# A selective scan: dt's maximum, B's diagonals and the mean's subtraction moved from VectorE to ScalarE and GpSimd

## The chip, the cores and the metric
One Trainium2 chip, 8 NeuronCores. Each core computes one sequence of the batch of 8, with no communication. The metric is the device time in microseconds of the slowest core. A core has TensorE (matmul, PE in the profile), VectorE (DVE), ScalarE (ACT), GpSimd (POOL) and SyncE (SP, here it only starts DMAs). Each works through its own queue of instructions in order; semaphores tie the queues together.

## The reference, cut to what matters
One layer of four parts: a Mamba block, a feed-forward block, attention, and the feed-forward block again, each with a layernorm ahead of it and a residual. Only the Mamba block is touched:
```python
# x: [2048 tokens, 1024] per core, after layernorm (x - mean) / sqrt(var + eps)
xb, zb = split(x @ in_proj_w)                 # 2048 channels each
xb = silu(conv4(xb)); zb = silu(zb)
dt, B, C = split(xb @ x_proj_w)               # 128, 16, 16
dt = softplus(dt @ dt_proj_w + dt_proj_b)     # per token and channel
h = exp(dt * A) * h + dt * B * xb             # 16 states per channel, scan over tokens
y = sum_n(C * h) + D * xb
out = (y * zb) @ out_proj_w
```

## The kernel before
The 2048 tokens are cut into four **quarters** q of 512, and the 2048 channels into 16 blocks c of 128. A **step** s = 16 q + c scans one block over one quarter; there are 64 steps. A step has 8 **slots** p, one for each pair of the 16 states (P = 8 s + p).

Work of one slot: ScalarE makes the two decays exp(dt A) of the pair after next (L910). TensorE multiplies the transposed v = dt * xb with diagonal matrices of B into PSUM (L921), for the next pair. VectorE runs the two scans of the pair (`tensor_tensor_scan`, L944), which read the decay from SBUF and the input from PSUM. After every second pair GpSimd copies the four last states for the next quarter (L956) and multiplies the four states with C (L959, 128x2048); TensorE sums those products over the states with identity matmuls (L1002) two slots later, in its queue behind the inputs of the next pair. VectorE multiplies the sum of a step with the gate in slot 3 of the next one (L1012). There are four buffers for states of two pairs, two for products.

dt of the next step is made inside a step: in slot 0 a matmul into a bank of PSUM (L853) and three passes on ScalarE: Relu (L857), Exp (L861), Ln (L865). They use softplus(u) = max(u, ln(1 + exp(min(u, 40)))), where min(u, 40) comes as 40 - relu(40 - u). In slot 2 VectorE takes the maximum with u, read from the bank (L875), which frees the bank, and GpSimd multiplies with xb for v (L880). In slot 4 TensorE transposes v (L890).

Between these, a list of **pieces** is spread over the slots of a step: projections of the next quarter (8 matmuls each, L587 and L685), gates, the output projection of the last quarter (L789, with the addition of x on VectorE, L803), and, in steps 0 to 2 of a quarter, the layernorm of the next. In its slot a piece comes last. The layernorm's eight tiles are applied in steps 1 and 2, four each: in quarter 0 in slots 0, 1, 4 and 6, in quarters 1 and 2 in slots 4 to 7. For one tile ScalarE copies x from SBUF to a PSUM bank (L562), VectorE subtracts the mean there (L568) and multiplies with 1/std into bf16 (L571). Step 14 of a quarter holds the x projection of the next, and at its end the 32 diagonal blocks of B (`dg`) in one VectorE operation (L761, 128x4096). In quarter 3 the pieces are passes of ScalarE over the feed-forward weights (|w|, L842, four a step), whose tiles SyncE loads into two buffers.

Three PSUM banks serve matmul pieces in turn (`take_bank`, `drop_bank`); if all three are held, late work is emitted early to free one. GpSimd's queue also starts weight-casting DMAs in slot 1 (L315): in steps 0 to 22, and then in every second step up to 30 (steps 0 to 2 have another in slot 5).

## Time and profile before
| | us |
|---|---|
| median of 3 runs | 3261.96 (3252.79 to 3271.25) |
| the profiled execution | 3267.86 |
| its slowest core (1), first to last instruction | 3266.2 |
| mean granted TensorE clock of that core | 0.885 of full speed |
| Mamba block, last gate product L1012 | starts at 1684.7 |

The profile was taken on core 1, and all rows below are that core's. Idle time stands behind an instruction in square brackets, with what ended it. "x4" is four instructions merged into one row. A row of the windows gives the stretch (start:end), its length, then the busy time (and instructions) of PE, PEld (weight loads), DVE, ACT and POOL, the granted clock, the DMA share and GB/s. Busy time on GpSimd there includes the starting of DMAs.

### The profile page before, as it was taken

To read this page: it belongs to the slowest core of one execution; us is meant where nothing else is said; L and a number is where in the kernel's file an instruction comes from. 1 tells how busy PE (TensorE), PEld (TensorE's weight loads), DVE (VectorE), ACT (ScalarE), POOL (GpSimd) and SP (SyncE) were. 2 spreads that over 40 slices of the span, in tenths; PEclk is the share of its full clock that TensorE was granted. 3 is DMA by queue.
4 is the path that set the end of the run, shared out by engine and by line. 5 is a ranking of instruction groups with operands and counts; after the bars stand their busy time and mean duration, and the time that the engine had idled before them with its cause. 6 is when DMAs were issued, how large, how long until landed. Compare 5 with 4: busy or idle time off the path is not lost.

```text
span 3266.2 us, 47261 instructions; the slowest of 8 cores (3212.5 to 3266.2 us)
## 1 busy us (share of the span) xinstructions
PE 2492.8 (76%) x16368; PEld 1159.3 (35%) x16368; DVE 1874.4 (57%) x1924; ACT 1863.5 (57%) x2713; POOL 1247.2 (38%) x622
## 2 busy tenths in 40 slices
PE   5555887678876876765564899899746887799999
PEld 2212332233322333322221344344534663344444
DVE  3267998799979999798853200421367765311001
ACT  2355886578866887788842653653222333563543
POOL 1246896588866887677740200200110000200000
PEclk8867998799988998877777899999878998899999
DMA  5567344645433112443344122131100112114323
GB/s 134 136 108 99 101 107 123 144 110 106 95 119 104 56 59 75 151 132 106 105 125 158 52 78 75 56 122 62 42 7 20 37 37 68 42 62 116 97 74 104
DMA packets 122616, 294.39 MB, mean 90 GB/s; under 512 B 16304, under 2 KB 24944, under 8 KB 119296
## 3 DMA queue, kind: packets, MB, share of 16 engines
q1 hardware_dynamic: 118480, 252.27, 25.3%
q0 software_dynamic: 3904, 39.09, 8.1%
q8 instruction: 137, 2.24, 0.3%
q14 instruction: 95, 0.78, 0.1%
HBM read 304.12 MB, written 60.00 MB: 111 GB/s over the span
## 4 chain that ended last, share of the span: by engine, by line
PE 50%; DVE 17%; ACT 13%; issue 10%; DMA 7%; SPq 1%; POOL 1%; DVEq 0%; ACTq 0%; POOLq 0%
PE ps L1403 13%; PE ps L1438 13%; DVE X L944 10%; ACT AR L910 6%; PE ps L1567 5%; PE ps L587 4%; PE ps L1002 4%; PE ps L789 2%; PE ps L921 2%; PE ps L1722 1%; ACT L910 1%; DVE AR L1263 1%; DMA AR<-x_fm 1%; PE ps L685 1%; DMA AR<-ip_bf 1%
## 5 line engine op out<-in xcount | busy, mean ns | idle before, releaser
L944 DVE TENSOR_TENSOR_SCAN X<-AR,ps 128x512 bf16<-128x512 f32 x1024 | 1208.9, 1244 | 132.6 <-PE ps L921 95.2
L959 POOL TENSOR_TENSOR AR<-X 128x2048 bf16<-128x2048 bf16 x256 | 1040.4, 4064 | 87.7 <-DVE X L944 81.1
L910 ACT ACTIVATE AR<-AR 128x512 f32<-128x512 f32 x1024 | 654.7, 711 | 6.5 <-DVE X L944 5.7
L921 PE MATMUL ps<-AR 64*128 64x128 bf16 x4096 | 221.8, 234 | 397.8 <-DVE X L944 373.4
L1403 PE MATMUL ps<-AR 128*128 128x512 bf16 x2048 | 463.4, 390 | 20.8 <-ACT AR L1331 13.4
L1438 PE MATMUL ps<-AR 128*128 128x512 bf16 x2048 | 445.1, 380 | 7.2 <-ACT AR L1331 7.2
L1194 POOL TENSOR_TENSOR AR<-X 128x512 f32<-128x512 f32 x8 | 10.1, 1264 | 1079.7 <-DVE AR L1263 689.1
L1460 DVE TENSOR_TENSOR X<-AR,X 128x512 f32<-128x512 f32 x64 | 43.6, 692 | 652.6 <-ACT AR L1452 652.6
L921 PEld LDWEIGHTS ps<-AR 64*128 64x128 bf16 x4096 | 134.4, 100 | 573.0 <-issue 571.6
L1002 PE MATMUL ps<-AR 128*128 128x512 bf16 x1024 | 323.3, 447 | 4.6 <-POOL AR L959 4.6
L1331 ACT ACTIVATE AR<-AR 128x1024 bf16<-128x1024 bf16 x256 | 258.0, 1046 | 117.0 <-DMA AR<-w2c 111.7
L587 PE MATMUL ps<-X,AR 128*128 128x512 bf16 x1024 | 280.6, 424 | 53.6 <-DMA AR<-ip_bf 27.5
L1403 PEld LDWEIGHTS ps<-AR 128*128 128x128 bf16 x2048 | 204.9, 100 | 282.3 <-issue 54.8
L1438 PEld LDWEIGHTS ps<-AR 128*128 128x128 bf16 x2048 | 200.4, 98 | 251.3 <-issue 11.8
L1567 PE MATMUL ps<-AR 128*128 128x256 bf16 x1536 | 199.4, 292 | 89.3 <-DVE AR L1584 31.3
L1413 ACT ACTIVATE AR<-ps,AR 128x1024 bf16<-128x1024 f32 x128 | 153.9, 1204 | 147.2 <-PE ps L1403 146.7
L1567 PEld LDWEIGHTS ps<-AR 128*128 128x128 bf16 x1536 | 155.6, 104 | 122.3 <-issue 94.6
L587 PEld LDWEIGHTS ps<-X,AR 128*128 128x128 bf16 x1024 | 106.2, 108 | 201.0 <-issue 113.5
L1452 ACT ACTIVATE AR<-ps,AR 128x512 f32<-128x512 f32 x64 | 46.3, 774 | 177.4 <-PE ps L1438 177.4
L956 POOL CAST AR<-X 128x4 f32<-128x4 bf16 x192 | 35.9, 187 | 279.5 <-DVE X L944 269.9
L1002 PEld LDWEIGHTS ps<-AR 128*128 128x128 bf16 x1024 | 94.5, 108 | 133.1 <-issue 62.3
L789 PE MATMUL ps<-AR 128*128 128x512 bf16 x512 | 129.7, 404 | 12.0 <-DMA AR<-op_bf 7.2
(136 smaller groups left out, 2493.9 us busy)
## 6 DMA issues: line engine op xcount, KB each, us to landing
X<-w SPq DMA_DIRECT2D x64, 512.0 KB, 3.7
AR<-w1c SPq DMA_DIRECT2D x128, 256.0 KB, 2.6
AR<-w2c SPq DMA_DIRECT2D x128, 256.0 KB, 3.1
AR<-ip_bf SPq DMA_DIRECT2D x112, 256.0 KB, 4.1
AR<-x_fm SPq DMA_DIRECT2D x80, 256.0 KB, 5.6
AR<-op_bf SPq DMA_DIRECT2D x32, 512.0 KB, 6.4
AR<-cdg SPq DMA_DIRECT2D x48, 256.0 KB, 3.5
X<-ip_pk SPq DMA_DIRECT2D x16, 512.0 KB, 3.7
```

The costliest lines, as they stand in the source:

```text
L587: f = lambda e, k=k: e.matmul(st["b"][1], wi[i][:, k, :], xn[q % 2][:, k, :], start=(k == 0), stop=(k == 7))
L789: f = lambda e, k=k: e.matmul(st["b"][1], wo[i][:, k, :], yz[(16 * q + k) % NYZ], start=(k == 0), stop=(k == 15))
L910: f = lambda e, n=n: e.activation(out=dec[P % 4][:, n, :], in_=dtt[s % 2], func=AF.Exp, scale=av[:, c, 2 * p + n:2 * p + n + 1])
L921: f = lambda e, tb=tb, h=h: e.matmul(self.bank(2 * (P % 2) + h)[:, tb * 128:tb * 128 + 128], vT[s % 2][64 * h:64 * h + 64, tb * 128:tb * 1 ...
L944: f = lambda e, n=n, init=init: e.tensor_tensor_scan(out=hh[J % 4][:, 2 * (P % 2) + n, :], data0=dec[P % 4][:, n, :], data1=src[:, :, n], ...
L959: S["hc", J] = tk("gp", lambda e: e.tensor_tensor(out=hc[J % 2], in0=hh[J % 4], in1=cbc[q % 2][:, 4 * j:4 * j + 4, :], op=ALU.mult))
L1002: f = lambda e, n=n: e.matmul(py, self.ident[:], hc[J % 2][:, n, :], start=False, stop=(j == 3 and n == 3))
L1331: u_ready[n] = tk("act", lambda e: e.sign(out=flat, in_=flat))
L1403: f = lambda e, k=k: e.matmul(pp[:, ch * 512:ch * 512 + 512], wu[n % NW][:, k, :], xn_h[:, k, ch * 512:ch * 512 + 512], start=(k == 0), st ...
L1413: ev[m] = tk("act", lambda e: e.activation(out=hact[:, m, :], in_=pp, func=AF.Gelu, scale=self.al1_t[:, m:m + 1], bias=self.b1_t[:, m:m + 1]))
L1438: e.matmul(pp[:, ch * 512:ch * 512 + 512], wu[n % NW][:, k, :], hact[:, kk, ch * 512:ch * 512 + 512], start=(kk == 0), stop=(kk == 31)))
L1567: f = lambda e, k=k: e.matmul(pb[:, 0:256], wts[i][:, j, k * 128:(k + 1) * 128], xu(w)[:, k, :], start=(k == 0), stop=(k == 7))
```

## The change
Three pieces of work leave VectorE.
1. softplus as a sum: u is at most 40 or not, so max(u, ln(1 + exp(min(u, 40)))) is written as relu(u - 40) + ln(1 + exp(min(u, 40))). ScalarE makes relu(u - 40) with a second Relu from the same bank (`zb`, one buffer, so it waits for the last step's addition), the bank is free after it, and GpSimd adds (L879 after the change) instead of VectorE's maximum.
2. B's diagonals: four operations of 128x1024 in place of one of 128x4096, each a piece of its own, on GpSimd from quarter 1 on (L759 after). A pair of states waits only for its quarter of them.
3. The mean: in quarters 1 to 3 GpSimd subtracts it in place in the SBUF tile of x (L561 after), and VectorE multiplies from there (L565 after). ScalarE's copy and the PSUM bank go.

```diff
         zb = alloc([128, TQ], F32)          # new
...
             def apply(k):
                 def main():
                     xk, ld, i = st["n", k]
-                    if q == 0:
-                        src = xk
-                        need("ve", ld)
-                    else:
-                        bi, src = take_bank()
-                        need("act", ld, bank_done[bi])
-                        c = tk("act", lambda e: e.activation(
-                            out=src, in_=xk, func=AF.Copy))
-                        r_xs.free[i] = (c,)
-                        need("ve", c)
-                    need("ve", S["ln_stat"], S.get(("z_in", q - 2)),
+                    eng = "ve" if q == 0 else "gp"
+                    need(eng, ld, S["ln_stat"])
+                    t = tk(eng, lambda e: e.tensor_tensor(
+                        out=xk, in0=xk, in1=mean, op=ALU.subtract))
+                    need("ve", t, S.get(("z_in", q - 2)),
                          S.get(("x_in", q - 2)))
                     t = tk("ve", lambda e: e.tensor_tensor(
-                        out=src, in0=src, in1=mean, op=ALU.subtract))
-                    need("ve", t)
-                    t = tk("ve", lambda e: e.tensor_tensor(
-                        out=xn[q % 2][:, k, :], in0=src, in1=rstd,
+                        out=xn[q % 2][:, k, :], in0=xk, in1=rstd,
                         op=ALU.mult))
                     if q > 0:
-                        drop_bank(bi, t)
+                        r_xs.free[i] = (t,)
...
-                S["dg", q] = tk("ve", lambda e: e.tensor_tensor(
-                    out=dg[q % 2].rearrange("p g (c n) -> p g c n", n=2),
+            def diag(i):
+                def main():
+                    eng = "ve" if q == 0 else "gp"
+                    need(eng, S["bt"], S.get(("inp_last", q - 2)))
+                    S["dg", q, i] = tk(eng, lambda e: e.tensor_tensor(
+                        out=dg[q % 2][:, 8 * i:8 * i + 8, :]
...
-            need("act", p, S.get(("v", s - 2)))
+            need("act", p, S.get(("v", s - 2)), S.get(("dt", s - 1)))
+            do("act", lambda e: e.activation(
+                out=zb, in_=pb, func=AF.Relu, bias=pdtb[:, c:c + 1]))
             t = tk("act", lambda e: e.activation(
                 out=dtt[b], in_=pb, func=AF.Relu, scale=-1.0,
                 bias=ndtb[:, c:c + 1]))
+            drop_bank(bi, t)
...
-            S["dt", s] = tk("ve", lambda e: e.scalar_tensor_tensor(
-                out=dtt[b], in0=pb, scalar=self.dtb_t[:, c:c + 1],
-                in1=dtt[b], op0=ALU.add, op1=ALU.max))
-            drop_bank(bi, S["dt", s])
+            need("gp", S["dt_ln", s])
+            S["dt", s] = tk("gp", lambda e: e.tensor_tensor(
+                out=dtt[b], in0=zb, in1=dtt[b], op=ALU.add))
...
-            need("pe", S["vT", s], S["dg", q], S.get(("scan", P - 2)))
+            need("pe", S["vT", s], S["dg", q, p // 2], S.get(("scan", P - 2)))
```

The order on GpSimd in step 17 (quarter 1) from slot 1 to slot 7, first before the change. `L956` and `L959` are the carry and the product of two pairs, `L880` is v, `c_ve` the wait for the scans.
```order
L956 CAST AR<-X 128x4 [waits c_ve,m_cb1,c_pe]
L959 TENSOR_TENSOR AR<-X 128x2048
L880 TENSOR_TENSOR AR<-AR 128x512 [waits c_ve,c_act]
L956 CAST AR<-X 128x4 [waits c_ve,c_pe]
L959 TENSOR_TENSOR AR<-X 128x2048
L956 CAST AR<-X 128x4 [waits c_ve,c_pe]
L959 TENSOR_TENSOR AR<-X 128x2048
L956 CAST AR<-X 128x4 [waits c_ve,c_pe]
L959 TENSOR_TENSOR AR<-X 128x2048
```
Now the same stretch after it, from slot 2 on: `L879` is dt's addition, `L882` v, `L958` and `L961` carry and product, `L561` the subtractions of slots 4, 5, 6 and 7.
```order
L879 TENSOR_TENSOR AR<-AR 128x512 [waits c_act]
L882 TENSOR_TENSOR AR<-AR 128x512 [waits c_gp]
L958 CAST AR<-X 128x4 [waits c_ve,c_pe]
L961 TENSOR_TENSOR AR<-X 128x2048
L561 TENSOR_TENSOR AR<-AR 128x512 [waits m_xs0]
L958 CAST AR<-X 128x4 [waits c_ve,c_pe]
L961 TENSOR_TENSOR AR<-X 128x2048
L561 TENSOR_TENSOR AR<-AR 128x512 [waits m_xs1]
L561 TENSOR_TENSOR AR<-AR 128x512 [waits m_xs2]
L958 CAST AR<-X 128x4 [waits c_ve,c_pe]
L961 TENSOR_TENSOR AR<-X 128x2048
L561 TENSOR_TENSOR AR<-AR 128x512 [waits m_xs3]
```
The subtraction of an odd slot stands behind the product of the pairs that end in this slot; that of slot 6 follows the one of slot 5 with nothing between.

VectorE in the same slots 4 to 6 after the change: `L946` are the scans, `L565` the multiplies, `L805` an addition of the output projection.
```order
L946 SCALAR_TENSOR_TENSOR X<-AR,ps 128x512 [waits c_act]
L565 TENSOR_TENSOR X<-AR 128x512 [waits c_gp]
L946 SCALAR_TENSOR_TENSOR X<-AR,ps 128x512 [waits c_pe,c_act]
L946 SCALAR_TENSOR_TENSOR X<-AR,ps 128x512 [waits c_act]
L805 TENSOR_TENSOR AR<-ps,AR 128x512 [waits m_xs3]
L565 TENSOR_TENSOR X<-AR 128x512 [waits c_gp]
L946 SCALAR_TENSOR_TENSOR X<-AR,ps 128x512 [waits c_pe,c_act]
```
Each multiply stands between two pairs of scans, and waits for GpSimd; before, a subtraction and a multiply stood at each of these places, and the first waited for ScalarE.

GpSimd at the end of step 14, from slot 3 on, after the change: `L759` are the four blocks of diagonals.
```order
L958 CAST AR<-X 128x4 [waits c_ve,c_pe]
L961 TENSOR_TENSOR AR<-X 128x2048
L759 TENSOR_TENSOR AR<-AR 128x1024 [waits c_ve]
L958 CAST AR<-X 128x4 [waits c_ve,c_pe]
L961 TENSOR_TENSOR AR<-X 128x2048
L759 TENSOR_TENSOR AR<-AR 128x1024 x2
L958 CAST AR<-X 128x4 [waits c_ve,c_pe]
L961 TENSOR_TENSOR AR<-X 128x2048
L759 TENSOR_TENSOR AR<-AR 128x1024
```
They are spread over slots 4 to 7, between the products; before, no diagonal stood in this queue.

## Rows read from the trace of the kernel before

**Rows 1.** The page, groups of instructions: busy, mean ns, idle before and its releaser.
```profile
L944 DVE TENSOR_TENSOR_SCAN X<-AR,ps 128x512 bf16<-128x512 f32 x1024 | 1208.9, 1244 | 132.6 <-PE ps L921 95.2
L959 POOL TENSOR_TENSOR AR<-X 128x2048 bf16<-128x2048 bf16 x256 | 1040.4, 4064 | 87.7 <-DVE X L944 81.1
```

**Rows 2.** Windows: steps 6-13, 19-29, 35-45, 14-15, 46-47, 17-18, 52-62.
```profile
338.70:495.50 156.80, 128.03 (x1004) 56.14 (x1002) 155.24 (x153) 140.71 (x237) 146.73 (x80) 0.97 0.43 105
648.20:877.40 229.20, 184.45 (x1365) 78.70 (x1363) 222.33 (x202) 189.10 (x313) 198.53 (x105) 0.93 0.49 105
1025.60:1252.80 227.20, 181.77 (x1369) 78.29 (x1366) 221.87 (x202) 189.16 (x313) 196.55 (x98) 0.94 0.21 62
495.50:543.30 47.80, 30.47 (x238) 12.96 (x237) 44.41 (x41) 35.45 (x53) 36.80 (x20) 0.86 0.55 143
1252.80:1301.80 49.00, 30.39 (x238) 13.09 (x238) 45.98 (x40) 35.51 (x53) 35.96 (x18) 0.86 0.31 101
577.10:648.20 71.10, 44.10 (x278) 17.94 (x276) 54.36 (x58) 37.35 (x57) 39.06 (x21) 0.75 0.64 148
1404.10:1657.00 252.90, 144.18 (x1089) 61.23 (x1089) 223.32 (x200) 216.72 (x339) 191.12 (x55) 0.74 0.33 107
```

**Rows 3.** Timeline of GpSimd in step 9 (start, us, instruction).
```profile
401.26 0.54 POOL L315 DMA_DIRECT2D w1c<-w1pk  x1
401.89 0.19 POOL L956 CAST AR<-X 128x4 f32<-128x4 bf16 x1
402.04 4.07 POOL L959 TENSOR_TENSOR AR<-X 128x2048 bf16<-128x2048 bf16 x1
406.07 1.16 POOL L880 TENSOR_TENSOR AR<-AR 128x512 bf16<-128x512 f32 x1
407.17 0.19 POOL L956 CAST AR<-X 128x4 f32<-128x4 bf16 x1
...
412.04 0.19 POOL L956 CAST AR<-X 128x4 f32<-128x4 bf16 x1 [0.66 <-DVE X L944]
```

**Rows 4.** Groups by line from 0 to 1500 us.
```profile
L875 DVE SCALAR_TENSOR_TENSOR AR<-ps,AR 128x512 f32<-128x512 f32 x57 | 41.4, 726 | 0.0
...
L857 ACT ACTIVATE AR<-ps,AR 128x512 f32<-128x512 f32 x58 | 39.2, 676 | 68.3 <-PE ps L853 68.2
...
L568 DVE TENSOR_TENSOR ps<-ps,AR 128x512 f32<-128x512 f32 x24 | 16.5, 689 | 27.5 <-ACT ps L562 27.5
```

**Rows 5.** Timeline of GpSimd in the first feed-forward stage.
```profile
1797.80 1.26 POOL L1194 TENSOR_TENSOR AR<-X 128x512 f32<-128x512 f32 x1 [115.22 <-DVE AR L1263]
1799.20 5.48 POOL L1198 TENSOR_TENSOR AR<-AR,X 128x512 f32<-128x512 f32 x4
```

**Rows 6.** Timelines of VectorE, then GpSimd, in step 33 (quarter 2).
```profile
979.53 0.70 DVE L568 TENSOR_TENSOR ps<-ps,AR 128x512 f32<-128x512 f32 x1 [2.00 <-ACT ps L562]
...
986.17 2.44 DVE L944 TENSOR_TENSOR_SCAN X<-AR,ps 128x512 bf16<-128x512 f32 x2
988.53 0.68 DVE L568 TENSOR_TENSOR ps<-ps,AR 128x512 f32<-128x512 f32 x1
...
989.92 2.44 DVE L944 TENSOR_TENSOR_SCAN X<-AR,ps 128x512 bf16<-128x512 f32 x2
...
983.58 0.19 POOL L956 CAST AR<-X 128x4 f32<-128x4 bf16 x1 [5.23 <-DVE X L944]
983.73 4.07 POOL L959 TENSOR_TENSOR AR<-X 128x2048 bf16<-128x2048 bf16 x1
```

**Rows 7.** Timelines: L761 at the start, and in step 46 beside GpSimd.
```profile
127.83 4.43 DVE L761 TENSOR_TENSOR AR<-AR 128x4096 bf16<-128x4096 bf16 x1
...
1271.37 5.51 DVE L761 TENSOR_TENSOR AR<-AR 128x4096 bf16<-128x4096 bf16 x1
...
1268.53 4.07 POOL L959 TENSOR_TENSOR AR<-X 128x2048 bf16<-128x2048 bf16 x1
```

**Rows 8.** Waits from 1404 to 1657 us: total, times, longest.
```profile
ACT X L842 <- DMA X<-w: 30.4, 11, 4.3
```

More of the change, by code:

```diff
@@ L356, in _mamba @@
         dtt = [alloc([128, TQ], F32) for _ in range(2)]
+        zb = alloc([128, TQ], F32)
         vv = alloc([128, TQ], BF16)
@@ L367, in _mamba @@
         ndtb = alloc([128, 16], F32)
+        pdtb = alloc([128, 16], F32)
         c40 = alloc([128, 1], F32)
@@ L391, in _mamba @@
             op0=ALU.mult, op1=ALU.add))
+        do("ve", lambda e: e.tensor_scalar(
+            out=pdtb, in0=self.dtb_t, scalar1=-40.0, scalar2=None,
+            op0=ALU.add))
         do("ve", lambda e: e.tensor_copy(
@@ L433, in take_bank @@
                 flush_add()
-            if all(bank_held) and late_dt:
-                late_dt.pop()()
             i = min((b for b in range(3) if not bank_held[b]),
@@ L753, in b_tr @@
                 S["bcr_used"] = p
-                need("ve", p)
+                need("ve", p, S.get(("dg", q - 1, 3)))
                 t = tk("ve", lambda e: e.tensor_copy(
@@ L759, in b_tr @@
                 drop_bank(bi, t)
-                need("ve", t, S.get(("inp_last", q - 2)))
-                S["dg", q] = tk("ve", lambda e: e.tensor_tensor(
-                    out=dg[q % 2].rearrange("p g (c n) -> p g c n", n=2),
-                    in0=id64.unsqueeze(1).unsqueeze(3)
-                    .broadcast_to([128, 32, 64, 2]),
-                    in1=bt.rearrange("p g (t n) -> p (g t) n", n=2)
-                    .unsqueeze(2).broadcast_to([128, 32, 64, 2]),
-                    op=ALU.mult))
+                S["bt"] = t
+            def diag(i):
[4 more added lines that the diff above has]
+                        out=dg[q % 2][:, 8 * i:8 * i + 8, :]
+                        .rearrange("p g (c n) -> p g c n", n=2),
+                        in0=id64.unsqueeze(1).unsqueeze(3)
+                        .broadcast_to([128, 8, 64, 2]),
+                        in1=bt[:, 2 * i:2 * i + 2, :]
+                        .rearrange("p g (t n) -> p (g t) n", n=2)
+                        .unsqueeze(2).broadcast_to([128, 8, 64, 2]),
+                        op=ALU.mult))
+                return main
             none = lambda: None
@@ L771, in xproj_pieces @@
                     (none, mm(1, 0, 8, 128, 160, 32)),
-                    (none, mm(1, 8, 16, 128, 160, 32)), (none, b_tr)]
+                    (none, mm(1, 8, 16, 128, 160, 32)), (none, b_tr),
+                    *((none, diag(i)) for i in range(4))]
         def out_pieces(q, m):
```

4 lines of the change are left out of this document (1 added, 3 removed).

## The prediction
> **What bounds the kernel now.** I read four views, in this order. The page's table of groups first [rows 1]: the scans are VectorE's largest group and the products of states with C GpSimd's, both over a stage that ends at about 1690 us of 3266; shares over the whole span say little about it. So the question is who limits one scan step. The windows second [rows 2]: in the eight dense steps of quarter 0 VectorE is busy 155.24 of 156.80 us, in the eleven of quarters 1 and 2 222.33 of 229.20 and 221.87 of 227.20. VectorE sets the pace there, at 19.4 us a step in quarter 0 and 20.2 in quarters 1 and 2 (busy time over steps). But the same rows give GpSimd 146.73 of 156.80, and 198.53 and 196.55: its room is 1 to 3 us a step. In quarter 3 (1404 to 1657) VectorE has room: ScalarE is busy 216.72 of 252.90 us and waits another 30.4 for the weight tiles of L842 [rows 8], 247.1 together, so ScalarE sets that pace. The timeline third: in a dense step GpSimd runs from one instruction into the next, with one hole of 0.66 us [rows 3]. The timeline of the normalisation fourth [rows 6], below.
>
> **The change part by part, against the profiled execution.**
>
> *dt's maximum, dense steps.* VectorE loses one operation of 726 ns per step [rows 4]; operations overlap their neighbours by some 0.08, so 0.65 is saved. GpSimd gains an addition of two float32 tensors of 128x512. Its price is that of the same shape elsewhere: four chained ones take 5.48 us, and the first, of 1.26 us, is followed by the next after 1.40 (1799.20 less 1797.80), since each waits for the one before [rows 5]. The product v waits for this addition in the same way, so I take 1.40. GpSimd's step from [rows 3]: four times 4.18 (401.89 to 406.07), 1.10 for v (406.07 to 407.17), 0.63 for a weight cast where there is one (401.26 to 401.89): 18.45 with a cast, 17.82 without. With 1.40 it is 19.85 and 19.22. VectorE's is 18.75 in quarter 0, 19.55 later. So GpSimd becomes the bound in quarter 0, where all steps have a cast, and in the casting half of quarter 1; elsewhere VectorE stays it by 0.3.
> Quarter 0: 8 x 19.85 = 158.8 against 156.8, +2.0. Quarter 1: 7 x 19.85 + 4 x 19.55 plus today's 6.9 of idle time = 224.1 against 229.2, -5.1. Quarter 2: 11 x 0.65 = -7.2. Two engines this close to each other lose something to each other's lateness: the sums on TensorE stand in front of the next inputs and wait for GpSimd. I take 0.15 for each of 30 steps, +4.3. Together **-6**; from -19.5 (30 x 0.65, GpSimd never late) to +9.
>
> *The Relu added on ScalarE.* One of 676 ns per step [rows 4]. In the dense steps ScalarE has 2 us of room. In quarter 3 it has none: busy and waiting make 247.1 of 252.9 us. The wait there (11 times, up to 4.3) hangs on ScalarE's own last pass over the buffer, and the Relu stands at the step's start, outside of that stretch, so it isn't absorbed: 13 steps x 0.67 = **+9**. VectorE's saving is worth nothing there. Bounds: 0 (the wait shrinks by as much) and 9.
>
> *B's diagonals.* VectorE loses three of 5.5 us with 1.23 of GpSimd's product still running at the start [rows 7]. GpSimd gains twelve of 1024 bfloat16 elements: half of the 2048 of L959, 4.06/2 = 2.03, with a start 2.1. High end: the float32 rate, 2 x 1.26 = 2.53. The broadcast pairs have no row nearer; low end 2.03. They stand between the products of pairs 3 to 7 of step 14 (the last order below the diff). Steps 14 and 15 take 47.80 us in quarter 0, 49.00 in quarter 2 [rows 2]. GpSimd's work in both: 8 x 4.18 + 2 x (1.40 + 1.10) + 4 x 2.1 + 0.6 = 47.4, of which about 2 is still outstanding when step 0 begins. So about 46, against 47.8 to 49: three times -2.5, **-7.5**. With the dear diagonals -2.5; if GpSimd hid them all, 3 x 7 = -21.
>
> *The other steps with a scan limited by waits* (steps 0 to 3 of three quarters, 14 in all with two of quarter 0): 0.65 each is 9, of which DMA waits swallow some: **-7**. *The start*: the addition lies on the only path to the first scan, **+1**. The first diagonals stay on VectorE.
>
> *The mean's subtraction.* 24 tiles (eight for each next quarter). Before: ScalarE copies x into a bank, VectorE subtracts and multiplies [rows 6]. The hole between scans is then 0.70 + 0.69 less overlaps = 1.30 (scan end to scan start around 988.53: 1.3) plus the wait for the copy, 27.5 us over 24 [rows 4]. Sum: 24 x 1.30 + 27.5 = 58.7 us.
> After: VectorE's multiply waits for GpSimd's subtraction, and that stands behind the product of the last pair of scans. The product can't start before those scans end. So, counted from the end of an odd pair's scans: 4.2 for carry and product (983.58 to 987.80 in [rows 6]), 1.26 subtraction, 0.14 for the semaphore [rows 5], 0.69 multiply: 6.3. A tile in an odd slot costs all of it, since VectorE can only do its multiply next; in an even slot one pair of scans (2.3 to 2.45) runs meanwhile, 4.0 is left, and 3.3 in slot 4, where the gate's product (0.67) covers more. In quarter 0's two steps the tiles lie in slots 0, 1, 4 and 6: 4.0 + 6.3 + 3.3 + 4.0 = 17.6. In quarters 1 and 2 they lie in 4, 5, 6, 7: 3.3 + 6.3 + 0.7 (its subtraction is long done) + 6.3 = 16.6. There one more thing: behind the subtraction of slot 5 the one of slot 6 stands ready, starts at once, and the multiply of slot 5 reads two SBUF tensors. What that costs is in [rows 7]: L761, also with two SBUF inputs, takes 4.43 alone and 5.51 when a GpSimd product started before it has 1.23 left. So the multiply waits out the subtraction, 1.26: 17.8.
> The Trainium skill (SBUF — State Buffer, "SBUF: two separate sides") has this as a rule: a VectorE operation with two SBUF inputs and a GpSimd operation exclude each other for a whole instruction, whoever is first. The trace agrees by that 1.08. Without the rule the sum would be 5 us lower. It also says why a copy into PSUM was no waste: L568 reads the bank and only one SBUF tensor.
> After: 2 x 17.6 + 4 x 17.8 = 106.4; less 58.7 is +47.7. Longer holes cover some later waits of scans for TensorE, so **+43**. Behind the waiting multiply stand the next scans, behind those TensorE's next inputs and GpSimd's next product: nothing else can run. Bounds: +20 (the holes fall together with other waits of these steps; VectorE is idle 16.7 of 71.1 us in steps 17 and 18 [rows 2]) to +55. ScalarE's 24 copies (0.6) go; it has room there.
>
> **Sum.** 43 - 6 - 7.5 - 7 + 1 + 9 = +32.5. The profiled execution took 3267.9 us (span 3266.2 on its slowest core, 1.7 around it); 3300.4 is its counterpart. It lies 5.9 above the median of 3261.96, so I forecast **3295**.
>
> **Rivals.**
> *GpSimd is the bound everywhere.* For it: 30 steps in which its work would be within 0.6 us of the step. If each late product costs TensorE and VectorE 0.5 more a step (+15) and the diagonals cost 2.53 (+5), and the holes are +55, it is 3325. Against it: TensorE is busy only 128 of 156.8 us and can catch up.
> *A wash.* The holes cost half (+22), since steps 17 and 18 already have 16.7 us of idle time on VectorE, and quarter 3's wait takes the Relu in (0): 22 - 6 - 7.5 - 7 + 1 = +2.5, 3264.
> *VectorE's relief decides, faster.* In all 30 dense steps 0.65 (-19.5), at the diagonals 3 x -7 = -21, elsewhere -9, while subtractions stay hidden (0) and the Relu too: 3212. It decides if the addition costs GpSimd under 1.1 instead of 1.40 (its step then under VectorE's even with a cast) and if product and subtraction together fit under one pair of scans, 5.5 in 2.4. The second contradicts [rows 6], so this needs GpSimd to be ahead of its queue, which it can't be, as it waits for the scans.
>
> **How the numbers follow.** Forecast 0.55, GpSimd bound everywhere 0.17, wash 0.18, faster 0.10. About 0.5%, 16 us, is what a measurement of this kernel can tell from no change: 3246 to 3278 is "same". The forecast lies above it; of the wash a sixth falls out on the fast side, and the fast rival all but wholly. Faster 0.11, same 0.17, slower 0.72. The range of eight in ten leaves out the fast rival and the far tail of the other: 3252 (wash with the dense steps at -19.5) to 3330 (rival one and a little more).
>
> **What the changed profile would show.** The holes between scans around the multiply: 6.3 in odd slots, 106 in sum, ended by GpSimd's subtraction; if they are under 80, that step is wrong. GpSimd's addition at 1.26 and its dense steps without a hole, quarter 0's step at 19.9. Diagonals at 2.1. Steps 14 and 15 at 46. Quarter 3's step 0.67 longer, with ScalarE's wait unchanged at 2.8 a step. The prediction fails if the tiles' holes were already filled by others' waits, or if GpSimd's lateness adds up rather than being taken back in each step.

## The result: a little slower, and where the time went

The changed kernel took 3291.36 us (median of 8), the kernel before, run beside it, 3264.59. The ratio is 1.0081, with a 95% interval of 1.0045 to 1.0117: slower by 0.8%. With one die of the chip at a lower clock some runs were up to 8% longer: they are in the two medians, not in the ratios of this document, and of the kernel called "no sub" the table below has only the four cores of the other die. The forecast was 3295 against a before of 3261.96, a ratio of 1.0101. The profiled execution took 3281.5 us, span 3279.9 on core 2; before it was 3267.9 and 3266.2 on core 1.

The page of the changed kernel, the groups that answer to [rows 1] (L946 are the scans, L961 the products with C, L912 the decays):
```profile
L946 DVE TENSOR_TENSOR_SCAN X<-AR,ps 128x512 bf16<-128x512 f32 x1024 | 1206.5, 1244 | 159.3 <-PE ps L923 83.8
L961 POOL TENSOR_TENSOR AR<-X 128x2048 bf16<-128x2048 bf16 x256 | 1040.6, 4065 | 82.8 <-DVE X L946 79.6
L912 ACT ACTIVATE AR<-AR 128x512 f32<-128x512 f32 x1024 | 654.3, 711 | 57.5 <-DVE X L946 56.6
```
The work of the two large groups is as before; what grew is VectorE's idle time, from 132.6 to 159.3 us ahead of the scans, and more in a row that this page doesn't show: 89.9 us ahead of the multiplies of the layernorm (L565), where 27.5 stood ahead of its subtractions [rows 4]. The growth has a place. The windows of core 2 for the same steps as in [rows 2], in the same order:
```profile
343.30:503.50 160.20, 127.55 (x990) 56.88 (x1009) 155.69 (x145) 145.90 (x245) 157.48 (x88) 0.96 0.49 103
666.00:886.10 220.10, 172.80 (x1331) 76.86 (x1356) 215.00 (x190) 191.47 (x320) 208.48 (x114) 0.95 0.46 107
1048.60:1270.30 221.70, 172.78 (x1331) 76.66 (x1356) 215.06 (x191) 191.98 (x320) 205.90 (x108) 0.95 0.19 59
503.50:549.40 45.90, 29.94 (x234) 12.90 (x238) 37.97 (x37) 36.61 (x55) 45.47 (x26) 0.85 0.59 149
1270.30:1315.20 44.90, 29.97 (x234) 13.38 (x238) 39.28 (x36) 37.14 (x55) 44.01 (x25) 0.83 0.31 116
584.30:666.00 81.70, 42.90 (x280) 18.33 (x283) 49.25 (x49) 37.28 (x55) 53.49 (x32) 0.75 0.51 132
1413.50:1676.60 263.10, 134.78 (x1068) 59.26 (x1089) 215.99 (x190) 223.28 (x350) 204.95 (x66) 0.79 0.31 104
```
In quarters 1 and 2 eleven dense steps now take 220.1 and 221.7 us, down from 229.2 and 227.2; quarter 0's eight take 160.2, up from 156.8, with GpSimd busy 157.48 of them. Steps 17 and 18 take 81.7 instead of 71.1 although VectorE and TensorE's matmuls are busy for less time in them and ScalarE for the same (37.28 us for 37.35), and steps 52 to 62 take 263.1 instead of 252.9.

VectorE in step 17 of the changed kernel, a timeline (start, us, instruction, in brackets the idle time and what ended it; L565 are the multiplies):
```profile
613.39 1.66 DVE L565 TENSOR_TENSOR X<-AR 128x512 bf16<-128x512 f32 x1 [5.13 <-POOL AR L561]
614.98 2.44 DVE L946 TENSOR_TENSOR_SCAN X<-AR,ps 128x512 bf16<-128x512 f32 x2
617.34 0.66 DVE L565 TENSOR_TENSOR X<-AR 128x512 bf16<-128x512 f32 x1
617.92 2.44 DVE L946 TENSOR_TENSOR_SCAN X<-AR,ps 128x512 bf16<-128x512 f32 x2
626.08 0.69 DVE L565 TENSOR_TENSOR X<-AR 128x512 bf16<-128x512 f32 x1 [5.72 <-POOL AR L561]
```
GpSimd in the same time (L958 carry, L961 product, L561 subtraction):
```profile
608.02 4.05 POOL L961 TENSOR_TENSOR AR<-X 128x2048 bf16<-128x2048 bf16 x1
612.02 2.48 POOL L561 TENSOR_TENSOR AR<-AR 128x512 f32<-128x512 f32 x2
620.56 0.19 POOL L958 CAST AR<-X 128x4 f32<-128x4 bf16 x1 [6.05 <-DVE X L946]
620.70 4.05 POOL L961 TENSOR_TENSOR AR<-X 128x2048 bf16<-128x2048 bf16 x1
624.71 1.27 POOL L561 TENSOR_TENSOR AR<-AR 128x512 f32<-128x512 f32 x1
```
The product starts when the scans of the odd slot have ended, the subtraction stands behind it (612.02, 624.71), and VectorE waits 5.13 and 5.72 us. GpSimd's next product then waits 6.05 us for VectorE (620.56): both engines stand still in turn. The multiply at 613.39 takes 1.66 us instead of 0.66: the two subtractions on GpSimd run until 614.50, and it ends 0.55 us behind them.

To tell cores apart from kernels, the table gives for each kernel, from its one profiled execution, the median over its cores of the time from the first scan of the first step to the first scan behind the last. "End of last scan" counts from the start of the execution; the first scan starts at 142 to 144 us, in "no sub" at 149. "Ratio" is the time of the whole kernel over that of the kernel before. "Ahead" and "best" are explained with their experiments.

| steps | before | after | no sub | sub only | dt only | diag only | ahead | best |
|---|---|---|---|---|---|---|---|---|
| 0 | 48.2 | 40.5 | 40.1 | 48.6 | 39.9 | 49.5 | 40.0 | 40.2 |
| 1-2 (layernorm) | 65.1 | 75.6 | 66.5 | 75.0 | 65.8 | 65.6 | 57.4 | 57.4 |
| 3-5 | 79.4 | 62.7 | 67.5 | 68.4 | 66.8 | 74.4 | 61.2 | 61.4 |
| 6-13 (dense) | 156.9 | 160.9 | 162.0 | 157.5 | 162.9 | 160.7 | 165.1 | 162.1 |
| 14-15 | 47.0 | 45.8 | 45.8 | 47.0 | 48.0 | 44.7 | 45.7 | 46.4 |
| 17-18 (layernorm) | 68.3 | 81.7 | 72.6 | 82.2 | 66.4 | 68.6 | 71.7 | 69.7 |
| 19-29 (dense) | 227.5 | 220.7 | 223.3 | 225.9 | 222.5 | 226.6 | 222.3 | 222.0 |
| 30-31 | 48.4 | 50.1 | 51.5 | 48.7 | 49.5 | 50.2 | 49.5 | 50.7 |
| 33-34 (layernorm) | 63.2 | 79.0 | 64.4 | 78.6 | 62.8 | 63.1 | 65.9 | 62.4 |
| 35-45 (dense) | 226.5 | 220.8 | 221.8 | 226.6 | 220.3 | 225.9 | 221.6 | 220.3 |
| 46-47 | 49.0 | 45.4 | 45.4 | 48.7 | 49.2 | 45.2 | 45.4 | 45.0 |
| 52-62 | 253.9 | 261.2 | 260.9 | 253.5 | 261.5 | 253.8 | 262.1 | 254.3 |
| end of last scan | 1663.2 | 1678.2 | 1661.2 | 1694.2 | 1641.7 | 1658.5 | 1636.8 | 1627.6 |
| ratio | 1 | 1.0081 | 0.9933 | 1.0104 | 0.9964 | 1.0009 | 0.9962 | 0.9883 |

What follows the scans took 1581.6 to 1587.5 us in all kernels, so the difference is made ahead of their end. The ends of the last scan are medians of one execution and the ratios go by the slowest core, so the two can differ by 10 us and more: the changed kernel's scans end 15.0 us later, its ratio makes it 26.

### The profile page after: what moved, and what is told of

Its sections match the earlier page's. It is cut to its first block, busy times and chain, and to the rows that moved or that the text cites. A ratio compares the mean times of both kernels' runs of the same rounds, so it can differ in the third digit from the quotient of the medians.

```text
span 3279.9 us, 47035 instructions; the slowest of 8 cores (3248.1 to 3279.9 us)
## 1 busy us (share of the span) xinstructions
PE 2446.5 (75%) x16130; PEld 1156.9 (35%) x16368; DVE 1812.9 (55%) x1837; ACT 1887.0 (58%) x2753; POOL 1376.4 (42%) x722
## 4 chain that ended last, share of the span: by engine, by line
PE 45%; DVE 14%; ACT 14%; issue 11%; POOL 7%; DMA 7%; SPq 1%; DVEq 0%; ACTq 0%; POOLq 0%; another core or an unknown queue 0%
PE ps L1405 13%; PE ps L1440 13%; DVE X L946 9%; ACT AR L912 6%; POOL AR L961 5%; PE ps L1569 5%; PE ps L1004 2%; PE ps L581 2%; DMA AR<-ip_bf 1%; PE ps L679 1%; DVE AR L1265 1%; PE ps L1724 1%; ACT L912 1%; DMA X<-w 1%; PE ps L791 1%
## 5 line engine op out<-in xcount | busy, mean ns | idle before, releaser
L946 DVE TENSOR_TENSOR_SCAN X<-AR,ps 128x512 bf16<-128x512 f32 x1024 | 1206.5, 1244 | 159.3 <-PE ps L923 83.8
L961 POOL TENSOR_TENSOR AR<-X 128x2048 bf16<-128x2048 bf16 x256 | 1040.6, 4065 | 82.8 <-DVE X L946 79.6
L912 ACT ACTIVATE AR<-AR 128x512 f32<-128x512 f32 x1024 | 654.3, 711 | 57.5 <-DVE X L946 56.6
L1405 PE MATMUL ps<-AR 128*128 128x512 bf16 x2005 | 457.8, 388 | 22.0 <-ACT AR L1333 13.3
L1440 PE MATMUL ps<-AR 128*128 128x512 bf16 x2008 | 443.2, 380 | 7.5 <-ACT AR L1333 5.4
L1004 PE MATMUL ps<-AR 128*128 128x512 bf16 x951 | 304.6, 445 | 44.5 <-POOL AR L958 22.4
L581 PE MATMUL ps<-X,AR 128*128 128x512 bf16 x995 | 260.7, 405 | 52.9 <-DMA AR<-ip_bf 32.0
L791 PE MATMUL ps<-AR 128*128 128x512 bf16 x505 | 130.7, 409 | 11.3 <-DMA AR<-op_bf 9.8
L679 PE MATMUL ps<-AR 128*128 128x512 bf16 x493 | 120.3, 385 | 17.2 <-ACT AR L641 7.2
```

The source lines that it names most:

```text
L581: f = lambda e, k=k: e.matmul(st["b"][1], wi[i][:, k, :], xn[q % 2][:, k, :], start=(k == 0), stop=(k == 7))
L791: f = lambda e, k=k: e.matmul(st["b"][1], wo[i][:, k, :], yz[(16 * q + k) % NYZ], start=(k == 0), stop=(k == 15))
L912: f = lambda e, n=n: e.activation(out=dec[P % 4][:, n, :], in_=dtt[s % 2], func=AF.Exp, scale=av[:, c, 2 * p + n:2 * p + n + 1])
L946: f = lambda e, n=n, init=init: e.tensor_tensor_scan(out=hh[J % 4][:, 2 * (P % 2) + n, :], data0=dec[P % 4][:, n, :], data1=src[:, :, n], ...
L961: S["hc", J] = tk("gp", lambda e: e.tensor_tensor(out=hc[J % 2], in0=hh[J % 4], in1=cbc[q % 2][:, 4 * j:4 * j + 4, :], op=ALU.mult))
L1004: f = lambda e, n=n: e.matmul(py, self.ident[:], hc[J % 2][:, n, :], start=False, stop=(j == 3 and n == 3))
```

## The experiments

### Each part by itself

**Without the subtraction** (the change, with ScalarE's copy and VectorE's subtraction put back):
```diff
-                    t = tk(eng, lambda e: e.tensor_tensor(
-                        out=xk, in0=xk, in1=mean, op=ALU.subtract))
+                        bi, src = take_bank()
+                        c = tk("act", lambda e: e.activation(
+                            out=src, in_=xk, func=AF.Copy))
...
+                        out=src, in0=src, in1=mean, op=ALU.subtract))
```


> The changed kernel with the mean's subtraction put back as before (copy to a bank on ScalarE, both operations on VectorE). My theory: the loss sits in the 24 holes of steps 1 and 2, so these six steps fall back from 79 to about 66 us a pair (13 less for each pair, 36 to 40 in all, less what the Relu and addition cost there) and what stays is dense steps -11, steps 14 and 15 -3, quarter 3 +7 to +10: 8 to 12 us faster than the kernel before, ratio 0.995 to 0.999. Rival, GpSimd's extra load (addition and diagonals) is what costs: the time stays at or above the kernel before, ratio 1.003 to 1.010.

**The subtraction only** (the kernel before with part 3 of the change, the edit above the other way round):
```diff
-                        out=src, in0=src, in1=mean, op=ALU.subtract))
+                    t = tk(eng, lambda e: e.tensor_tensor(
+                        out=xk, in0=xk, in1=mean, op=ALU.subtract))
```


> The kernel before with the mean's subtraction alone moved to GpSimd. My theory: the holes between scans at the 24 tiles go from 63 us in sum to about 110, so +40 to +47, ratio 1.012 to 1.015; more than the whole change. Rival, the holes come only with a GpSimd that is made busy by the addition: holes under 80 us and a ratio under 1.005.

**dt's sum only** (part 1 alone; VectorE makes all diagonals in one operation, as before):
```diff
-            S["dt", s] = tk("ve", lambda e: e.scalar_tensor_tensor(
-                out=dtt[b], in0=pb, scalar=self.dtb_t[:, c:c + 1],
-                in1=dtt[b], op0=ALU.add, op1=ALU.max))
+            S["dt", s] = tk("gp", lambda e: e.tensor_tensor(
+                out=dtt[b], in0=zb, in1=dtt[b], op=ALU.add))
```


> The kernel before with dt's maximum alone replaced by the second Relu and GpSimd's addition. My theory: dense steps of quarter 0 go to 20.0 us (+3 to +4 over eight), those of quarters 1 and 2 fall by 0.5 to 0.65 each (-11 to -14), steps 0 to 3 fall by 5 in all, quarter 3 from step 52 on rises by 0.67 a step (+7 to +9): -5 to -10 in all, ratio 0.997 to 0.9985. Rival, GpSimd as bound everywhere: dense steps of quarters 1 and 2 at 20.5 or more, ratio above 1.003.

**The diagonals only** (part 2 alone):
```diff
-                S["dg", q] = tk("ve", lambda e: e.tensor_tensor(
+                    eng = "ve" if q == 0 else "gp"
+                    S["dg", q, i] = tk(eng, lambda e: e.tensor_tensor(
```


> The kernel before with B's diagonals alone in four pieces on GpSimd. My theory: steps 14 and 15 become bound by GpSimd at 8 x 4.18 + 2 x 1.10 + 4 x 1.9 + 0.6 = 43.8 and some lateness, 44.5 to 45.5 against 47.0 to 49.0, so -3 to -4 for each of three quarters, -9 to -12 in all, ratio 0.996 to 0.9975. Rival, the diagonals only hide behind other waits there: under 3 us in all, ratio 0.999 to 1.001.

Measured: 0.9933 (0.9908 to 0.9957), 1.0104 (1.0079 to 1.0130), 0.9964 (0.9930 to 0.9999) and 1.0009 (0.9979 to 1.0039). So the sign is the subtraction's: with it alone the kernel is 1.0% slower, and leaving it out of the change makes 1.0081 into 0.9933, 1.5% or 48 us. The three parts alone add up to 0.77%, the whole change is 0.81%. Its cost sits in the six layernorm steps, 75.0, 82.2 and 78.6 us in the table against 65.1, 68.3 and 63.2.

dt's sum is a small gain, with an interval that all but reaches 1, although it costs 7.6 us in steps 52 to 62 and 6 in 6 to 13: it gains 5.0 and 6.2 in the dense steps of quarters 1 and 2, and 8.3 and 12.6 in steps 0 and 3 to 5, where I had expected 0.65 a step (below). Four to five of the 6 us in steps 6 to 13 are the addition's: a dense step of quarter 0 in which nothing else is waited for takes 20.0 us in every kernel that has it there and 19.4 in every other. All four ratios lie outside the ranges that I had given: the kernel without the subtraction and the one with dt's sum alone came out faster, the subtraction alone cost less, the diagonals gained less.

The diagonals missed: 2 to 4 us less in two of three places (44.7 against 47.0, 45.2 against 49.0), 1.8 more in steps 30 and 31, and nothing in the whole that the runs can tell. The step that had the one large operation does get shorter, step 30 from 26.4 to 22.7 us (22.3 in the changed kernel), but step 31 goes from 22.0 to 27.5 (27.9). In the changed kernel this is what VectorE does in step 31:
```profile
904.91 8.28 DVE L946 TENSOR_TENSOR_SCAN X<-AR,ps 128x512 bf16<-128x512 f32 x7
921.23 2.45 DVE L946 TENSOR_TENSOR_SCAN X<-AR,ps 128x512 bf16<-128x512 f32 x2 [8.04 <-PE ps L923]
924.55 2.45 DVE L946 TENSOR_TENSOR_SCAN X<-AR,ps 128x512 bf16<-128x512 f32 x2 [0.87 <-ACT AR L912]
```
It waits 8.04 us for TensorE's inputs. TensorE had waited in the same stretch for a tile of the input projection's weights; the waits of 908 to 937 us (total, times, longest):
```profile
DVE X L946 <- PE ps L923: 8.0, 1, 8.0
...
PE ps L581 <- DMA AR<-ip_bf: 5.4, 1, 5.4
```
What the diagonals gave in step 30 was handed over to this load. Without them on VectorE the 5.5 us are gone, but the next thing that is late is a transfer. In the kernel before no core waits for it in step 31, with the diagonals alone on GpSimd all eight do, 1.6 to 6.6 us.

### The lock of two SBUF readers

The change, with one more wait: GpSimd's next instruction behind a subtraction waits until VectorE has done the multiply. So no instruction of GpSimd runs beside these multiplies.
```diff
                     if q > 0:
                         r_xs.free[i] = (t,)
+                        need("gp", t)
```


> The changed kernel, where GpSimd's queue waits for each multiply of VectorE before its next instruction. In the changed profile six of the 24 multiplies take 1.66 us and not 0.69, just those behind which a GpSimd operation stood ready (slot 5 in quarters 1 and 2, slot 1 in quarter 0). My theory, one engine waits out the other's instruction when both want two SBUF inputs: now all 24 take 0.66 to 0.70, and the holes of slots 1 and 5 fall from 7.3 to 6.3, while GpSimd's next operation comes 0.7 later. Rival, these six are long for another reason (their place behind the addition L805 or behind a long product): they stay at 1.6.

It ran once, in 3275.27 us. Its multiplies by line, shortest, median and longest in ns:
```profile
L565 DVE TENSOR_TENSOR X<-AR x24: 664/692/693, 190.1 to 1035.9; 128x512 bf16<-128x512 f32 x24
```
And those of the changed kernel:
```profile
L565 DVE TENSOR_TENSOR X<-AR x24: 660/692/1669, 192.1 to 1048.0; 128x512 bf16<-128x512 f32 x24
...
  POOL AR L561: 89.9, 20
```
The longest falls from 1669 to 693 ns, and the sum of the 24 holes, on core 2 of both kernels, from 112.3 to 106.3 us, 6.0 for six multiplies of 0.97 each (a **hole** is the time from the end of the scan ahead of a multiply to the start of the scan behind it). What lengthens these multiplies is the GpSimd instruction beside them, and not their place or their data. This is the Trainium skill's rule (SBUF — State Buffer, "SBUF: two separate sides"), with this case's 0.66 and 1.66 us beside it.

### The place in the queue, not the engine

The same subtraction on GpSimd, but queued one tile ahead: the one of tile k + 1 is emitted with the multiply of tile k, so that it stands in front of the product that the next multiply would have waited for.
```diff
+            def sub(k):
+                xk, ld, i = st["n", k]
+                eng = "ve" if q == 0 else "gp"
+                need(eng, ld, S["ln_stat"])
+                st["t", k] = tk(eng, lambda e: e.tensor_tensor(
+                    out=xk, in0=xk, in1=mean, op=ALU.subtract))
...
             def apply(k):
                 def main():
+                    if ("t", k) not in st:
+                        sub(k)
+                    if q > 0 and k % 4 < 3:
+                        assert ("n", k + 1) in st
+                        sub(k + 1)
```


> The changed kernel with the subtractions of tiles 1 to 3 and 5 to 7 put into GpSimd's queue one tile earlier, in front of the product that they waited behind. My theory, the place in the queue makes the holes and not the work: steps 1 and 2 of each quarter fall from 76 to 82 us a pair to 66 to 71, 25 to 35 us less in all, ratio to the kernel before 0.992 to 1.000. Rival, the multiplies with two SBUF inputs collide with products that are then ready (4 us each): less than 10 us are won, ratio 1.005 or more.

Ratio 0.9962 (0.9940 to 0.9985), so against the change 1.2% faster, by the order of one instruction. Its multiplies, groups by line (busy, mean ns, idle before):
```profile
L572 DVE TENSOR_TENSOR X<-AR 128x512 bf16<-128x512 f32 x24 | 43.3, 1804 | 20.4 <-POOL AR L560 20.4
```
and the same by line, shortest, median and longest in ns:
```profile
L572 DVE TENSOR_TENSOR X<-AR x24: 659/1268/4581, 192.3 to 1007.1; 128x512 bf16<-128x512 f32 x24
```
The wait for GpSimd is 20.4 us where it was 89.9. The multiply's mean is 1804 ns where it was 930: it now falls beside GpSimd's long products, and the longest takes 4.58 us. So the lock takes back 21 us of the 69.5. The holes sum to 63.0 us, where the changed kernel had 112.3 and the kernel before 63.0. Steps 1 and 2 take 57.4 us, less than the 65.1 before the change: there the idea does pay. Steps 17 and 18 and 33 and 34, at 71.7 and 65.9, stay 3 us above what they were. Nor is the whole faster than the change without any subtraction on GpSimd (0.9933; the intervals overlap): the order takes the loss away, but the move itself pays in quarter 0's two steps alone.

### Where each part pays

**Mixed**: dt's sum in quarters 1 and 2 only, the diagonals on GpSimd, the old layernorm.
```diff
+            if q in (1, 2):
+                need("gp", t)
+                S["dt", s] = tk("gp", lambda e: e.tensor_tensor(
+                    out=dtt[b], in0=zb, in1=dtt[b], op=ALU.add))
+            else:
```
The branch that is left is VectorE's maximum; the same condition stands at the second Relu and at the early `drop_bank`.


> No subtraction on GpSimd, the diagonals on GpSimd, and the Relu with the addition only in quarters 1 and 2, VectorE's maximum in quarters 0 and 3. My theory: quarter 3 from step 52 on goes back to 254 us (from 261), dense steps of quarter 0 to 157 (from 161), quarters 1 and 2 keep their 5 to 6 each; whether step 0 keeps the 8 us that all kernels with the new form of dt show there is open. Ratio 0.992 to 0.997. Rival, the rise of quarter 3 doesn't come from ScalarE's Relu: it stays at 261.

**Mixed, with steps 0 to 5**:
```diff
-            if q in (1, 2):
+            if s < 6 or 16 <= s < 48:
```


> As the mix, with the new form of dt also in steps 0 to 5. If the early steps gain by it (step 0 at 40 and not 48 us, steps 3 to 5 at 63 and not 79), this one is 8 to 20 us faster than the mix, ratio 0.987 to 0.993; if the gain there was chance of the weight DMAs, the two are alike.

0.9971 (0.9946 to 0.9995) and 0.9945 (0.9909 to 0.9980). Both have steps 52 to 62 at 255.7 and 254.3 us, as the kernel before; every kernel with the second Relu there has 260.9 to 262.1. The term of quarter 3 is confirmed, for the sum form as a whole; no run has the Relu without the addition. The second moves steps 0 and 3 to 5 from 49.2 and 77.1 us to 40.3 and 62.3. Its ratio missed the range I had given (0.987 to 0.993), and the two intervals overlap: the 24 us of these steps don't all arrive at the end.

**Best**: the last one, with the subtraction ahead in quarter 0's two steps and the old layernorm for the others.
```diff
+                    if q == 1:
+                        if ("t", k) not in st:
+                            sub(k)
+                        if k % 4 < 3:
+                            sub(k + 1)
```


> Built from the parts that each did well: the mixed version before it (diagonals on GpSimd; the sum form of dt only in steps 0 to 5 and in quarters 1 and 2; VectorE's maximum elsewhere), and the subtraction on GpSimd, queued one tile ahead, in quarter 0's two steps alone, where the run with the subtraction ahead took 57.4 us for these two steps against 65.1 of the kernel before and 66.4 of the mixed version. Quarters 1 and 2 keep ScalarE's copy. My theory (what the subtraction costs is its place in GpSimd's queue, not the engine that does it): steps 1 and 2 take 57 to 59 us, the scan stage ends some 8 us earlier than the mixed version's 1635.8, and the whole is 0.990 to 0.9935 of the kernel before. Rival: the gain of those two steps is only borrowed, since the dense steps behind them take it back (in the run with the subtraction ahead, quarter 0's steps 6 to 13 took 165.1 against 160.5): ratio 0.9935 to 0.996, with steps 6 to 13 at 165.

0.9883 (0.9838 to 0.9927), 38 us faster than the kernel before and 65 than the change (1.0081 less 0.9883 is 0.0198). Steps 1 and 2 keep their 57.4; steps 6 to 13 take 162.1, 1.6 more than in the mixed version, so the rival is right only to that extent. The ratio is better than I expected, by more than the 8 us between the ends of the last scan explain; the intervals of the two versions overlap.

### The 8 and 17 us that nobody had promised

In steps 0 and 3 to 5 every kernel with dt's sum there had 40 and 61 to 68 us, and the others 48 to 50 and 68 to 79 (medians). Three kernels for it, all of them the kernel before with an edit in steps 0 to 5 only. **The sum form only there**:
```diff
+            if s < 6:
+                drop_bank(bi, t)
...
+            if s < 6:
+                need("gp", t)
+                S["dt", s] = tk("gp", lambda e: e.tensor_tensor(
+                    out=dtt[b], in0=zb, in1=dtt[b], op=ALU.add))
+            else:
```


> The kernel before with the sum form of dt in steps 0 to 5 alone; nothing else changed. All kernels with it so far took 40 us for step 0 (48 without it) and 62 to 67 for steps 3 to 5 (74 to 79 without it), far more than 0.65 a step. If that is due to these additions themselves: step 0 at 40, steps 3 to 5 at 62 to 67, of which the dense steps take back some, since the next instruction to wait for is the load of the input weights; ratio 0.993 to 0.997. If it needed the other parts as well: ratio 0.999 to 1.001.

**The same, the bank held** until the addition:
```diff
-            if s < 6:
-                drop_bank(bi, t)
...
                     out=dtt[b], in0=zb, in1=dtt[b], op=ALU.add))
+                drop_bank(bi, S["dt", s])
```


> As the run with the sum form in steps 0 to 5 alone, but the PSUM bank of dt is kept until the addition, as the maximum kept it, so that the pieces go to the same banks at the same time as in the kernel before. Theory A (the early release of the bank is what speeds these steps: the pieces' matmuls and the layernorm's tiles behind them start sooner): step 0 returns to 48 and steps 3 to 5 to 75 to 79, ratio 0.999 to 1.001. Theory B (the place of the maximum is what slowed them: VectorE, waiting for ScalarE's Ln in front of its scans): both keep the values of the run without the hold, ratio 0.993 to 0.997. Theory C (GpSimd's addition delays the weight casts behind it in the queue, and the loads of x and of the input weights get through first): the same values as B, but the starts of the cast transfers in step 0 are later than in the kernel before by the addition's wait.

**Only an idle addition**: the maximum stays on VectorE, and GpSimd adds a buffer to itself.
```diff
+            if s < 6:
+                need("gp", t, S["zb"])
+                S["zb"] = tk("gp", lambda e: e.tensor_tensor(
+                    out=zb, in0=zb, in1=zb, op=ALU.add))
```


> The kernel before, with VectorE's maximum kept in every step, and in steps 0 to 5 one more GpSimd addition of 128x512 float32 whose result nobody uses, at the place of dt's addition: behind the Ln, ahead of v. It stands ahead of the weight cast of step 0 and delays it as the real addition does. The bank is held as before. Theory C (what speeds step 0 and steps 3 to 5 is that the weight cast starts later against the loads of x, which both pass through the 16 DMA engines): step 0 at 40 us, steps 3 to 5 at 62 to 68, ratio 0.994 to 0.999 although the kernel does more work. Theory B (the maximum's place on VectorE slowed them): step 0 stays at 48, steps 3 to 5 at 75 to 80, ratio 1.000 to 1.003.

| | step 0 (cores' range) | 1-2 | 3-5 (range) | ratio |
|---|---|---|---|---|
| before | 48.2 (40.6 to 50.7) | 65.1 | 79.4 (60.9 to 83.4) | 1 |
| the sum form there | 40.2 (39.2 to 42.1) | 66.0 | 62.3 (62.1 to 79.7) | 0.9940 (0.9913 to 0.9967) |
| and the bank held | 39.6 (37.8 to 41.4) | 69.5 | 67.4 (62.1 to 78.1) | 0.9989 (0.9965 to 1.0013) |
| idle addition | 41.7 (39.3 to 46.8) | 64.7 | 63.0 (61.9 to 76.8) | no interval; 3248.2 and 3253.0 us beside a mean of 3259.0 for the kernel before |

An addition that computes nothing brings 6.5 of the 8 us and 16 of the 17. With the bank held the short step 0 stays, so it isn't the freed bank (A); with the maximum still on VectorE it comes all the same, so it isn't the maximum's place (B). What the idle addition does change is when things start. In every core of a kernel without an addition the cast of weights behind v starts 2.6 us after the one ahead of it (both of `ip_pk`, in GpSimd's queue), with the idle addition 3.6, with dt's 4.0. Step 0 took under 44 us in 6 of the 32 cores of the kernels with 2.6 (before, sub only, diag only, mixed), in 5 of the 8 with 3.6, and in all 68 with 4.0.

What step 0 waits for is the loads of x. ScalarE's squares of x (L519 before), first of the kernel before, core 1, whose first scan starts at 143.1:
```profile
165.19 0.63 ACT L519 ACTIVATE AR<-AR 128x512 bf16<-128x512 f32 x1 [12.01 <-DMA AR<-x_fm]
...
176.45 0.63 ACT L519 ACTIVATE AR<-AR 128x512 bf16<-128x512 f32 x1 [8.06 <-DMA AR<-x_fm]
```
and of the kernel with the idle addition (there L521), core 4, whose first scan starts at 147.4:
```profile
167.90 1.29 ACT L521 ACTIVATE AR<-AR 128x512 bf16<-128x512 f32 x2 [10.46 <-DMA AR<-x_fm]
...
171.02 0.63 ACT L521 ACTIVATE AR<-AR 128x512 bf16<-128x512 f32 x1 [0.60 <-DMA AR<-x_fm]
172.80 0.63 ACT L521 ACTIVATE AR<-AR 128x512 bf16<-128x512 f32 x1 [1.16 <-DMA AR<-x_fm]
```
The last tile of x is there 33.3 us behind the first scan before and 25.4 in this one. Yet two of the eight cores of the kernel before had the short step 0 as well (42.3 and 40.6), and three with the idle addition took 46 to 47: it looks like a race between casts of 1 MB and loads of 256 KB, both served by the core's 16 DMA engines, which a microsecond tips. That is an argument and not shown. The mark that I had named for theory C did not come: the cast behind v starts 2.6 us ahead of the first scan in all kernels, since that scan waits for the same v. Counted from the loads of x on SyncE's queue it starts later with the idle addition by the median (7.4 us against 6.2), but the cores overlap (6.3 to 9.1 against 5.1 to 8.8), and within the kernel with the idle addition the later cores are not the quicker ones (8.0 and 9.1 us go with a step 0 of 46.7 and 45.9). So which start decides stays open.

Part of the gain in steps 3 to 5 is handed back. TensorE waits there for a tile of the input projection's weights, in step 5 on core 1 of the kernel before (total, times, longest):
```profile
PE ps L587 <- DMA AR<-ip_bf: 19.4, 2, 18.0
```
On core 6 of the same kernel step 5 has no such wait and takes 20.3 us, but step 6 then takes 25.2, with 4.4 of it. That is most of why steps 6 to 13 take 162.0 us with the idle addition and 156.9 before, although nothing differs in them. Over steps 0 to 13 the medians are 351.2 before, 334.9 with the idle addition, 329.7 with the sum form and 336.3 with the bank held. That holding the bank costs 3.5 us in steps 1 and 2 fits theory A there, but doesn't make up the whole difference of the two ratios: the held version's 0.9989 is what A had predicted, its step 0 is not, and the rest stays open.

## Why the prediction was right

The forecast was slower with 0.72, at 3295, by the wait of VectorE for a subtraction that stands behind a product. The experiments bear the sign and its cause out: the subtraction alone gives the loss, and the place in the queue alone takes it away. The size is less firm, and that the sum came so near (1.0101 forecast, 1.0081 measured) is in part luck, since terms missed in both directions. The ratio of the runs makes the difference 26 us (15 to 38), the two profiled executions 13.6, of which 19.4 lie ahead of the last scan's end, and 5.7 come back behind it. A single profiled pair can't tell more, when runs of one kernel differ by 20 us and more. Step by step, with the difference after less before of the two profiled cores, and of the medians of the table:

- **The layernorm steps**, expected +43: +32.9 (11.5, 10.6, 10.8) on the profiled cores, +39.7 (10.5, 13.4, 15.8) by the medians, 34 by the ratio of the subtraction alone, 48 by those of the change with and without it. The holes: predicted 58.7 to 106.4, measured 63.0 to 112.3. The shapes are as in the prediction: 7.3 in slot 5, 6.3 in slot 7, 0.5 in slot 6, and 5.13 and 5.72 of waiting in the timelines. In slot 4 of quarters 1 and 2 the holes are 2.8 to 6.0 for a predicted 3.3; the longest is there because the subtraction itself waited 2.8 us for its tile of x. Missed: the lock strikes in quarter 0's slot 1 too (7.3 where 6.3 was predicted), where dt's addition stands right behind the subtraction: six times, not four, and at 0.97 rather than 1.26 each. With the subtraction alone, and no addition, these two multiplies take 0.69.
- **Dense steps**, expected -6: -11.1 (+3.4, -9.0, -5.5), by medians -8.5 (+4.0, -6.8, -5.7). GpSimd's step in quarter 0 is 20.0 us (160.2 over 8), predicted 19.85. The addition takes 1.27 and v follows 1.42 behind its start:
```profile
428.28 0.18 POOL L958 CAST AR<-X 128x4 f32<-128x4 bf16 x1
428.43 4.07 POOL L961 TENSOR_TENSOR AR<-X 128x2048 bf16<-128x2048 bf16 x1
432.45 1.27 POOL L879 TENSOR_TENSOR AR<-AR 128x512 f32<-128x512 f32 x1
433.87 1.16 POOL L882 TENSOR_TENSOR AR<-AR 128x512 bf16<-128x512 f32 x1
434.97 0.19 POOL L958 CAST AR<-X 128x4 f32<-128x4 bf16 x1
```
  The 0.15 a step that I added for lateness was the right size in quarter 0 (+3.4 against the +2.0 of the sum without it) and wasn't needed in quarters 1 and 2, where the prediction's own terms were -5.1 and -7.2, sum -12.3, and -12.5 came by the medians (-14.5 on the profiled cores).
- **Relu in quarter 3**, expected +9 for 13 steps, so 7.4 for the eleven from 52 to 62: +10.2, by medians +7.3. The medians give 0.66 a step, the Relu's own time. The wait for the weights did not shrink; on the profiled cores it grew by 4.0 while ScalarE's busy time grew by 6.6, and these two make up the 10.2. The waits of 1413 to 1677 us:
```profile
DVE X L946 <- ACT AR L912: 46.2, 21, 3.7
ACT X L844 <- DMA X<-w: 34.4, 11, 4.6
```
  ScalarE's wait is 34.4 (30.4 in [rows 8]), and VectorE waits 46.2 us for the decays, 22.3 more than the 23.9 before. As said, VectorE's saving is worth nothing there.
- **Diagonals and steps 14 and 15**, expected -7.5: -4.1 (-1.9, +1.8, -4.0), by medians -3.1. (The sum in the prediction has a slip: 47.4 less 2 is 45.4 and not 46, which makes the term nearer -9 than -7.5; likewise 30 x 0.15 is 4.5 and not 4.3.) A block took 1.9 us, where I had taken 2.1 and 2.03 as the low end. Steps 14, 30 and 46 each fell by 4.0 to 4.1 us; steps 15 and 31 gave 3.0 and 5.9 back (47 gave 0.5). In step 31 it is the load, which the prediction did not have; what it is in step 15 was not taken apart. Groups by line of the changed kernel, with the addition and the subtraction:
```profile
L879 POOL TENSOR_TENSOR AR<-AR 128x512 f32<-128x512 f32 x64 | 81.1, 1267 | 0.1
...
L561 POOL TENSOR_TENSOR AR<-AR 128x512 f32<-128x512 f32 x24 | 30.1, 1263 | 2.8 <-DMA AR<-x_fm 2.8
...
L759 POOL TENSOR_TENSOR AR<-AR 128x1024 bf16<-128x1024 bf16 x12 | 22.9, 1916 | 0.0
```
- **Other steps**, expected -7, and the start +1: the start +1.7. Step 0 gained 6.2 and steps 3 to 5 gained 2.3 on the profiled core, and 7.7 and 16.7 by the medians. With steps 16, 32 and 48 to 51 (+1.1, +1.6, -4.1) the profiled cores come to -9.9, near the forecast, but by another way: I took 0.65 a step off VectorE, and most of what came is the shift of the transfers (above), which made these steps faster on most cores. By the medians this is the term that was mis-sized. On the profiled core steps 3 to 5 still took 81.1 us, so this gain reached the slowest core only in part.

**The rivals.** GpSimd as the bound everywhere did not come, only in quarter 0, as forecast: quarters 1 and 2 are faster than before, with 11.6 and 15.8 us of room left to GpSimd over 11 steps. The wash needed half-price holes and a free Relu; the holes grew by 49.3 us where 47.7 was predicted, and the Relu was at full price. VectorE's relief did not decide, since the holes are there; the kernels without the long holes are the faster ones, and reach 0.9883.

## What to carry to other kernels

When work moves to an engine that consumes what the giver produces, ask what it stands behind in the new queue: an instruction of 1.26 us behind a product that waits for the scans cost VectorE 4.5 us a time (89.9 us in 20 waits), and the same instruction queued one tile ahead made the kernel 1.2% faster. Leaving it on its old engine did as much (1.5%), so a better place in the queue doesn't yet make the move pay. Try the parts of a change apart and in each stage apart: here each part paid in some stages and cost in others, and the choice by stage, with the subtraction ahead in one of them, took 1.0081 to 0.9883. And where loads and large casts share the DMA engines, look at several cores before a gain is put down to arithmetic: an addition that did nothing brought most of 8 us in one step, and the cores of one kernel differed by more than that.
